# First experts of a two-layer kernel: 15 slots of 128 places with one expert each become 12 slots of two 64-place halves with an expert each, in native fp32

## The reference

```
x = x + tanh(g_xattn[0]) * cross_attention_0(layernorm(x), context)     16 heads of 16
x = x + tanh(g_ffn[0])   * experts_0(layernorm(x))                      8 experts, one per token
x = x + tanh(g_xattn[1]) * cross_attention_1(layernorm(x), context)     keys and queries normalised
x = x + tanh(g_ffn[1])   * block_1(layernorm(x))                        causal attention, 16 + 3 expert tiles
```

```
route = sigmoid(x @ router_w)                 (8 values);  e = argmax(route)
y = (silu(x @ gate_w[e]) * (x @ up_w[e])) @ down_w[e] * route[e]
```

## Time and profile before

| | |
|---|---|
| median of 3 runs | 750.92 us (746.13 to 752.42) |
| the profiled execution's own time | 748.34 us |
| its span (first to last instruction) | 746.6 us |
| PE busy, share of the span | 721.7 us, 97% |
| DVE, ACT, POOL busy | 453.9, 368.3, 302.7 us |
| slot loop (first gate product to the last down product's end) | 101.2 to 186.9 us |
| second cross attention | about 195 to 283 us |

### The profile page before, as it was taken

The page is one execution under the profiler, slowest core; times in us unless marked ns, Lnnn a source line. Parts: engine busy times, 40 slices in busy tenths (PEclk is TensorE's granted clock), DMA queues, the critical chain, the costliest instruction groups (busy, mean ns, idle before and its releaser), DMA issues.

```text
span 746.6 us, 14041 instructions
## 1 busy us (share of the span) xinstructions
PE 721.7 (97%) x4675; PEld 605.9 (81%) x4676; DVE 453.9 (61%) x824; ACT 368.3 (49%) x860; POOL 302.7 (41%) x385
## 2 busy tenths in 40 slices
PE   8999989999879999999999999999999999999997
PEld 6887657888568788889998899988778888888886
DVE  6888577555598955544355443555566656666565
ACT  4888236664376854544445444454533232232323
POOL 3323265665578747223222232212334344344430
PEclk9999999999999999999999999999999999999999
DMA  8990121110300001011010110100014433434321
GB/s 288 417 355 2 29 73 48 42 56 31 111 16 15 23 2 36 22 36 53 26 35 21 35 51 27 63 1 22 22 50 135 115 104 113 126 98 119 117 88 57
DMA packets 24744, 57.53 MB, mean 77 GB/s; under 512 B 3568, under 2 KB 13296, under 8 KB 23680
## 3 DMA queue, kind: packets, MB, share of 16 engines
q1 hardware_dynamic: 23936, 54.90, 22.3%
q0 software_dynamic: 768, 2.10, 0.9%
HBM read 50.89 MB, written 6.09 MB: 76 GB/s over the span
## 4 chain that ended last, share of the span: by engine, by line
PE 81%; ACT 5%; DVE 5%; POOL 5%; issue 2%; DMA 1%; SPq 0%; DVEq 0%; ACTq 0%; POOLq 0%
PE PS L352 17%; PE PS L354 16%; PE PS L353 16%; PE PS L1869 7%; PE PS L1525 4%; PE PS L470 2%; PE PS L476 2%; PE PS L1875 2%; PE PS L514 2%; PE PS L1507 2%; PE PS L1504 2%; PE PS L1501 2%; PE PS L505 1%; POOL Z L851 1%; PE PS L527 1%
## 5 line engine op out<-in xcount | busy, mean ns | idle before, releaser
L1290 ACT ACTIVATE hhh<-hh 128x512 fp32r<-128x512 f32 x50 | 31.6, 632 | 103.6 <-DVE hh L1312 94.7
L352 PE MATMUL PS<-tTh,wh 128*128 128x512 f32 x200 | 78.3, 392 | 0.8 <-DVE tTl L670 0.5
L354 PE MATMUL PS<-tTh,wl 128*128 128x512 f32 x200 | 77.9, 389 | 0.0
L353 PE MATMUL PS<-tTl,wh 128*128 128x512 f32 x200 | 77.8, 389 | 0.0
L670 DVE TENSOR_TENSOR hhl<-hh,hhh 128x512 fp32r<-128x512 f32 x50 | 52.4, 1048 | 35.4 <-ACT hhh L1290 35.4
L2080 POOL CAST ah<-araw 128x512 fp32r<-128x512 f32 (+1 forms) x32 | 16.2, 506 | 134.4 <-PE PS L354 134.3
L1378 POOL CAST wh<-wraw 128x512 fp32r<-128x512 f32 (+1 forms) x50 | 26.1, 522 | 108.6 <-PE PS L354 108.6
L1978 ACT ACTIVATE sm<-sm,nmx 128x128 f32<-128x128 f32 x128 | 49.7, 390 | 37.7 <-DVE nmx L2041 37.7
L670 DVE TENSOR_TENSOR oTl<-PS,oTh 128x512 fp32r<-128x512 f32 x32 | 22.1, 691 | 71.6 <-ACT oTh L1972 71.6
L1380 POOL TENSOR_TENSOR wl<-wraw,wh 128x512 fp32r<-128x512 f32 (+1 forms) x50 | 58.1, 1161 | 8.4 <-POOL wh L1378 7.9
L1573 POOL TENSOR_TENSOR wgl<-WE,wgh 128x512 fp32r<-128x512 f32 x28 | 47.0, 1700 | 26.4 <-ACT wgh L1619 25.8
(11 more groups left out here) (278 smaller groups left out, 1969.0 us busy)
## 6 DMA issues: line engine op xcount, KB each, us to landing
WE<-moe SPq DMA_DIRECT2D x8, 1536.0 KB, 19.0
wraw<-moe SPq DMA_DIRECT2D x25, 384.0 KB, 3.0
araw<-attn SPq DMA_DIRECT2D x16, 384.0 KB, 3.0
cwb<-cw_d SPq DMA_DIRECT2D x20, 256.0 KB, 3.9
WX<-wx SPq DMA_DIRECT2D x4, 512.0 KB, 6.8
avraw<-attn_v SPq DMA_DIRECT2D x8, 256.0 KB
xs_d<-zeros SPq DMA_DIRECT2D x1, 1920.0 KB, 22.4
ys_d<-y_s SPq DMA_DIRECT2D x15, 128.0 KB, 1.7
```

Source lines behind the costliest of these rows:

```text
L352: nc.tensor.matmul(out, wh_, xh_, start=first, stop=False, **kw)
L353: nc.tensor.matmul(out, wh_, xl_, start=False, stop=False, **kw)
L354: return nc.tensor.matmul(out, wl_, xh_, start=False, stop=last, **kw)
L1290: nc.scalar.activation(hhh[half][:, :], hh[half][:, :], ACT.Copy).then_inc(s.hi_done, 1)
```

## The change

- There are 24 halves of 64 places. Each half has its own expert, and a slot is two neighbouring halves: 12 slots.
- Tokens are no longer split in high and low parts. Gate, up and down are native fp32 products. The first half's rows are the stationary operand of the strip of columns 0 to 63 and meet the first expert's weights, read in place from WE; the second half's rows use columns 64 to 127 and meet a copy (w2) of the second expert's weights. Both write to the same PSUM bank, on partitions 0 to 63 and 64 to 127.
- w2 has one buffer. ACT copies the gate part (two instructions), DVE the up part (two), POOL the down part (one of 1024 elements), each behind the product that last read it. The splitting work of ACT, DVE and POOL goes.
- Every engine that needs an expert reads its number from ex; PE now reads it twice a slot.
- The routing's small tensors are wider (16 thresholds, 24 halves), and POOL sets 17 constants more in the first attention.
- Behind the loop DVE adds row 0 and takes its moments ahead of normalising the last keys, row by row in another order; POOL takes each row's power behind gathers 2 and 3, gathers five rows ahead of the attention instead of six, and squares, queries and powers stand in another order in it. The moments of rows 4 to 7 come in two groups (POWERS has ("ln3", 4, 6) and ("ln3", 6, 8)).
- Fillers: 5 become 14 ahead of the last two key turns, 6 at the start of the second attention go, 4 come ahead of the second query squares. The wait for the turned keys moves to step -1.

```diff
-SLOTS = T // P + E0 - 1
+HP = P // 2
+HALVES = T // HP + E0
+SLOTS = HALVES // 2
...
-        xsT = [sb(f"xsT{i}", [P, C, P], F32R, e) for i in range(2)]
+        xsT = [sb(f"xsT{i}", [P, C, P], where=e) for i in range(2)]
...
-        xsTl = [sb(f"xsTl{i}", [P, C, P], F32R, e) for i in range(2)]
-        wgh = [sb(f"wgh{i}", [P, C, I0], F32R, e) for i in range(2)]
+        w2 = sb("w2", [P, EW], where=e)
...
             def query_squares(b):
+                out = bank("Q2", b)
+                if b == 1:
+                    fill(4, 4 + turn_no[L]["Q2", b] % 4)
                 pe.wait_ge(s.sq_done, b + 1)
-                out = bank("Q2", b)
                 for c in range(C):
...
-            pe.wait_ge(Es.kt_free, B)
-            fill(6, 7)
             for n in steps():
+                if n == -1:
+                    pe.wait_ge(Es.kt_free, B)
...
                 squares(0)
+                gather(EARLY + 1)
                 power(pool, "ln3", FIRST)
             normed(2)
             if L:
+                squares(1)
                 queries(0)
-                squares(1)
                 gather(MOST)
                 gather(MOST + 1)
-                queries(1)
             else:
                 residual(0)
             for n in range(B):
...
                     power(pool, "ln1", n + 3)
                 if not L and n == 2:
                     routing_constants()
-                if L and n == 1:
-                    power(pool, "ln3", EARLY)
+                if L and n in (1, 3):
+                    power(pool, "ln3", EARLY + n - 1)
                 if n + 3 < B:
                     normed(n + 3)
+                if L and n == 0:
+                    queries(1)
...
+            def single(j):
+                body(j, j % 2, (j - 3) // 2 if j % 2 else (j - 4) // 2)
             for j in range(3):
-                body(j, j % 2, (j - 3) // 2 if j % 2 else (j - 4) // 2)
+                single(j)
             pairs = (SLOTS - 5) // 2
             with eng.Fori(0, pairs) as i:
                 body(2 * i + 3, 1, i)
                 body(2 * i + 4, 0, i)
-            for j in (SLOTS - 2, SLOTS - 1):
-                body(j, j % 2, pairs)
+            for j in range(3 + 2 * pairs, SLOTS):
+                single(j)
+        def half_expert(eng, j, h):
+            return eng.value_load(ex[0:1, bass.ds(2 * j + h, 1)], min_val=0, max_val=E0 - 1)
+        def expert_part(e, a0, n):
+            return WE[:, bass.ds(e, 1), a0:a0 + n].rearrange("p a n -> p (a n)")
...
-            def up(j, par, mat, done):
-                out = PS[:, 2 * mat + par, :]
+            def up(e, j, par, mat, done):
                 for c in range(C):
-                    pe.wait_ge(s.w_high, 4 * j + 2 * mat + c + 1)
-                    nc.tensor.matmul(out, xsT[par][:, c, :], wgh[mat][:, c, :], start=(c == 0), stop=False)
-                    if mat == 0 and c == 0:
-                        pe.wait_ge(s.xt_low, j + 1)
-                    nc.tensor.matmul(out, xsTl[par][:, c, :], wgh[mat][:, c, :], start=False, stop=False)
-                for c in range(C):
-                    pe.wait_ge(s.w_low[(mat + c) % 2], 2 * j + mat + 1)
-                    m = nc.tensor.matmul(out, xsT[par][:, c, :], wgl[mat][:, c, :], start=False, stop=(c == C - 1))
+                    a0 = (mat * C + c) * I0
+                    out, x = PS[:, 2 * mat + par, :], xsT[par][:, c, :]
+                    nc.tensor.matmul(out[0:HP, :], x[:, 0:HP], expert_part(e, a0, I0), start=(c == 0), stop=(c == C - 1))
+                    pe.wait_ge((s.gate_copied, s.up_copied)[mat], 2 * j + c + 1)
+                    m = nc.tensor.matmul(out[HP:P, :], x[:, HP:P], w2[:, a0:a0 + I0], start=(c == 0), stop=(c == C - 1))
                 m.then_inc(done, 1)
...
-                e = pe.value_load(ex[0:1, bass.ds(j, 1)], min_val=0, max_val=E0 - 1)
+                e = half_expert(pe, j, 0)
                 pe.wait_ge(s.ht_ready, j + 1)
-                w = WE[:, bass.ds(e, 1), 2 * C * I0:EW].rearrange("p a (k n) -> p (a k) n", n=D)
                 src = hidden_rows(j)
                 for k in range(I0 // P):
                     if between is not None and k == I0 // P // 2:
                         between()
-                    m = nc.tensor.matmul(PS[:, 6 + par, 0:D], src[:, k, :], w[:, k, :], start=(k == 0), stop=(k == I0 // P - 1))
+                    a0 = 2 * C * I0 + k * D
+                    out = PS[:, 6 + par, 0:D]
+                    nc.tensor.matmul(out[0:HP, :], src[:, k, 0:HP], expert_part(e, a0, D), start=(k == 0), stop=(k == I0 // P - 1))
+                    if k == 0:
+                        pe.wait_ge(s.down_copied, j + 1)
+                    m = nc.tensor.matmul(out[HP:P, :], src[:, k, HP:P], w2[:, a0:a0 + D], start=(k == 0), stop=(k == I0 // P - 1))
                 m.then_inc(s.d_done, 1)
             def tile(j, par, i):
+                e = half_expert(pe, j, 0)
                 pe.wait_ge(s.xt_ready, j + 1)
-                up(j, par, 0, s.g_done)
+                up(e, j, par, 0, s.g_done)
                 if is_first(j):
-                    up(j, par, 1, s.u_done)
+                    up(e, j, par, 1, s.u_done)
...
-                    fill(5, 2)
+                    fill(14, 2)
...
-                e = None if is_last(j) else expert(j + 1)
+                e = None if is_last(j) else half_expert(act, j + 1, 1)
                 act.wait_ge(s.g_done, j + 1)
                 nc.scalar.activation(gs[par][:, :], PS[:, par, :], ACT.Silu).then_inc(s.silu_done, 1)
                 if is_first(j):
-                    weights(e, 0)
-                    act.wait_ge(s.u_done, 1)
-                    weights(e, 1)
+                    gate_copies(e)
                     hidden_columns(0)
                     columns(1, 1)
                     return
...
                     hidden_columns(j - 1)
                 if not is_last(j):
                     columns(j + 1, 1 - par)
-                    weights(e, 0)
-                    act.wait_ge(s.u_done, j + 1)
-                    weights(e, 1)
...
+                    gate_copies(e)
+            def gate_copies(e):
                 for c in range(C):
-                    nc.scalar.activation(wgh[mat][:, c, :], expert_columns(e, mat, c), ACT.Copy).then_inc(s.w_high, 1)
+                    nc.scalar.activation(w2[:, c * I0:(c + 1) * I0], expert_part(e, c * I0, I0), ACT.Copy).then_inc(s.gate_copied, 1)
             act.wait_ge(s.experts_done, 1)
             act.wait_ge(s.w_in, 16 * E0)
-            e = expert(0)
-            weights(e, 0)
-            weights(e, 1)
+            gate_copies(half_expert(act, 0, 1))
...
-            if b in (0, FIRST - 1, EARLY - 1, B - 1):
+            if b in (0, FIRST - 1, EARLY - 1, MOST - 1, B - 1):
...
+            def up_copies(e):
+                for a0 in (C * I0, (C + 1) * I0):
+                    v.tensor_copy(w2[:, a0:a0 + I0], expert_part(e, a0, I0)).then_inc(s.up_copied, 1)
             def tile(j, par, i):
-                e = None if is_last(j) else expert(j + 1)
-                if not is_first(j) and not is_last(j):
-                    low_columns(j + 1, 1 - par)
+                e = None if is_last(j) else half_expert(dve, j + 1, 1)
                 dve.wait_ge(s.u_done, j + 1)
                 dve.wait_ge(s.silu_done, j + 1)
                 v.tensor_tensor(hs[:, :], gs[par][:, :], PS[:, 2 + par, :], ALU.mult).then_inc(s.h_ready, 1)
                 if not is_last(j):
-                    low_gates(j + 1, e)
+                    up_copies(e)
                 if is_first(j):
                     keys_values(4, MOST)
                     output_rows(0, 0, 0)
-                    low_columns(1, 1)
-                    low_ups(1, e)
                     normalise_keys(dve, 0, MOST, 1)
                     return
                 if not is_second(j):
                     output_rows(j - 1, 1 - par, i + 1)
-                if not is_last(j):
-                    low_ups(j + 1, e)
             dve.wait_ge(s.experts_done, 1)
-            e = expert(0)
-            low_gates(0, e)
             keys_values(0, 1, False)
-            low_columns(0, 0)
-            low_ups(0, e)
+            dve.wait_ge(s.w_in, 16 * E0)
+            up_copies(half_expert(dve, 0, 1))
...
             def keys_power(b0, b1, group):
                 pool.wait_ge(s.kms_done, group)
                 nc.gpsimd.tensor_tensor(krs8[:, b0:b1], kms8[:, b0:b1], mhalf[:, b0:b1], ALU.pow).then_inc(s.krs_done, 1)
+            def down_copies(e):
+                nc.gpsimd.tensor_copy(w2[:, 2 * C * I0:EW], expert_part(e, 2 * C * I0, EW - 2 * C * I0)).then_inc(s.down_copied, 1)
+            def tile(j, par, i):
+                if is_first(j):
+                    keys_power(0, MOST, 1)
+                if not is_last(j):
+                    e = half_expert(pool, j + 1, 1)
+                    pool_wait(pool, s.d_done, j + 1)
+                    down_copies(e)
```

(42 more changed lines are left out.)

56 lines of the change are left out of this document (13 added, 43 removed).

## The result

The median after is 739.74 us (739.04 to 741.17, 4 runs), against 749.57 us (746.13 to 752.42, 4 runs) for the kernel before in the same comparison. The ratio is 0.987, 95% interval 0.985 to 0.990. In a second comparison, also of the unchanged kernel after, it was 0.988 (0.986 to 0.991). So the change saves some 9 to 10 us, 1.2 to 1.3%. The forecast was 741 (734 to 752).

The account below looks back on a forecast made before the run. TensorE was taken to bound the kernel, the loop costing slots times slot length. Loop -6.6 and head -3.2 made -9.8 on the profiled 748.3, 738.5; with the median 2.6 above, 741 us, range 734 to 752.

Parts of the forecast that it names:

- Strips: Slot loop's gate, up and down: two 64-column strips overlap fully, 0.43 us per instruction pair, 1.72 a product.
- The values product: Product at L527, sixteen native products in four 32-wide strips: took 1.07 us against 3.44 in series, read as full overlap.
- The mark to look for: Sign for the strips: gate rows starting 0.43 us apart in pairs, a gate of 1.72, a slot of 6.2 to 6.3.
- The rival prices of 0.54 and 0.86 a pair: Slot loop: strips overlap partly (757 us) or run in series (803 us); chance 0.12, of it 0.05 for series.
- Array changes: Slot loop: switching between strips and full width twice a slot costs 0.2 us each, bounds 0 and 0.4.
- Sequencer reads: Slot loop: TensorE's sequencer reading an expert twice a slot costs 0.1 us a slot, bound 0.3.
- The last slot: Slot 11, with four products and two hidden turns, takes 8.8 us; no wait for a weight copy was put down.
- Copies in the regular slots: Slot loop: ACT, DVE and POOL copies of w2 fit in 4.5 us, so TensorE never waits on them.
- Start of the loop: Before slot 1: the 1.30 us bank wait goes; first gate at 100.2, gate(1) at 110.6, 0.7 earlier.
- Head: Loop's end to second attention's first scores: gain 3.3 to 3.6 us, 0.3 taken back, -3.2 net; bounds 0 and -4.5.
- The first rival: Second attention gives the head's gain back, POOL's queries behind squares and gathers delaying the exponents: 744 us, chance 0.14.
- The loop's bounds: Range around the loop's -6.6 us: -12.2 with changes and reads at nothing, 0 with 0.4 a change, 0.3 a read.

Follow-up runs that it names:

- experiment 3: Changed kernel with both halves' products sent to one column strip, same number and size of products: 801.97 us, one run, slot 11.27.
- experiment 4: Changed kernel with 15 slots of 128 places, native fp32 products on the whole array, no halves or copies: 753.82 us, one run.
- Experiments 6 and 7: 6: changed kernel, second half's weight copies made twice in all slots but the first, 742.98 us; 7: changed kernel, two down-weight buffers, 741.19 us.
- experiment 10: Changed kernel with 5 fillers instead of 14 ahead of the last key turns and none ahead of the second query squares: median 742.39 us.

## Why the prediction was right, point by point

**Strips: right.** The values product gave the right reading, full overlap with both instructions of a native product, and experiment 3 shows it by its opposite. The mark to look for, pairs 0.43 apart, is there. The rival prices of 0.54 and 0.86 a pair fall.

**Array changes: the right order, slightly high.** 0.65 + 0.4 a slot were put down for transposes and changes. A slot of 6.12 less three products of 1.72 leaves 0.96, and the same sum for experiment 4's slot without strips 0.66, so the two changes cost 0.3 and not 0.4. The Trainium skill ("TensorEngine Tiling (Array Packing)", Tiling Modes) says that a change drains TensorE. The trace agrees that it isn't free, with the 0.17 us that the weight loads idle behind the transposes, but small.

**Sequencer reads: cost nothing.** 0.1 a slot was put down; the slot is 6.12, not 6.3. That is 1.66 over nine slots, changes included, to the good.

**The last slot: the step that failed.** The forecast said that a copy "has a slot less 1.72 us, 4.5 us, to finish", in every slot. That holds only while other products stand between two that use the buffer. The last slot took 9.96 from its gate to the loop's end instead of 8.8; with the second buffer it takes 8.47. It was hidden in the sum, because the regular slots were shorter: loop's end forecast at 180.3, measured at 180.09. Experiments 6 and 7 show both sides of it, a second copy makes it longer, a second buffer takes it away.

**Copies in the regular slots: right.** No wait on them. VectorE's two took 0.75 us as a rule, ScalarE's 1.15 and GpSimd's one 1.04, all well inside the bound of 4.5, and doubling them changed nothing.

**Start of the loop: right in kind.** The 1.30 went. The rest is 0.4 to 0.5 late: the first gate at 100.56 for 100.2, gate(1) at 111.09 for 110.6. Since like kernels differ by 3.4 us in when they reach the first gate, this part of the sum is neither borne out nor refuted.

**Head: mechanism right, size too large.** Put down as 3.5 to 3.6 less, with 0.3 given back; measured as 2.75 less with 1.1 given back, -1.7 net for a forecast of -3.2. Two terms were mis-sized. Row 0's add came a microsecond later than worked out from the gathers' median, 0.5 of it by the issue and 0.5 by the landing; what follows it took 5.7 for the 5.9 to 6.2 put down. And of the reordering inside the attention, costed at 0.3, the second power for rows 4 to 7 alone cost 0.9 at row 5. The first rival, gain given back in the attention, was thus partly true: 0.9 of the 1.1 for a reason that it didn't name, a second power in a chain where POOL has no gap. Its own reason, POOL's queries coming later, may have a share at row 3, where q_scale is 0.5 late; no experiment takes that order back alone. The clock stayed high, as forecast, and experiment 10 gives it a price.

**The sum.** -9.8 was forecast; the profiles give -8.6, the medians -9.8, the second comparison -8.7. Part of the agreement is luck: the head's forecast was 1.5 too good, the loop's 0.2 too small, and the two profiles differ in their low-clock stretches, which neither term describes. The step from the profile to the median is luck too. 2.6 was added, as for before; after's median stands 0.05 above its profiled execution, and its four runs have mean clocks of 0.995 to 1.000. And -9.8 by the medians is measured from 749.57, where the forecast started at 750.9. The loop's bounds are slightly off in the adding: -6.6 less 4.8 and 1.0 is -12.4, not -12.2, and the upper one comes to some 0.2 to 0.6 above no gain; the range stays as good as it was.

## What to carry to other kernels

Where work is padded to a tile per group, as here, half tiles in two column strips cut the padding, and what it costs is the strips' own small changes: 12 slots of 6.12 against 15 of 5.3. For a buffer that is refilled behind its reader, check the first and the last turn of the pipeline apart from the steady state; there the work that covers the refill is missing. An operation that is split in two for an earlier start can cost more in sum (0.70 and 0.72 for one of 1.03), and in a chain without a gap most of that comes back: 0.85 of 0.90 at row 5, 0.5 of 0.7 at row 3. And where a head waits for one transfer, its landing sets the pace, so a median over all such transfers is a weak price for the first.

## What the runs showed of the hardware

- Two 64-column strips with 512-column native products ran side by side with no loss: a pair of instructions per 0.43 us, and 0.86 when both use one strip.
- A wait ahead of a product of one strip stops the later products of the other strip too: after 176.77 the first strip's products stood still until 178.22, though their operands were ready.
- VectorE's two copies of 512 elements took 1.83 us in slot 0, with GpSimd's copy of 1.04 beside them (104.86 and 105.03 above), and 0.75 in a regular slot, where nothing of GpSimd's ran beside them.
- From the start of the last output's copy on VectorE (180.20 after, 187.14 before) to the first gather it was 3.0 us in all ten profiles of kernels with the new slot code (2.98 to 3.05), also in that of 15 slots without halves, and 2.4 in the two with the old code. What makes the difference is open.
- The first gather behind the loop landed 3.15 to 4.39 us behind its issue in ten profiles, by the start of the add that waits for it; the median of all eight gathers of before is 2.9.
